# Residual base finished by VectorE in one operation in place of one of ScalarE and one of GpSimd, with all five queues of a two-layer graph network ordered anew

## The reference, cut to what matters

```python
h = jnp.maximum(_layernorm(x), 0.0)
x = x + L @ (h @ W + b)                    # layer 0; L is the normalised adjacency + I
h = jnp.maximum(_layernorm(x), 0.0)        # layer 1 starts
# hypergraph convolution: out = D^-1 H B^-1 H^T (h @ W^T) + bias, H = (adj != 0)
t = relu(hconv(h, adj, W1, b1))            # 512 -> 1024
t = layer_norm(t, gamma, beta)
x = x + (hconv(t, adj, W2, b2) + h)        # 1024 -> 512, plus the layer's own input
```

## Time and profile before

| | us |
|---|---|
| time, median of 3 runs | 1917.77 (1917.34 to 1918.89) |
| time of the profiled execution | 1915.19 |
| its span, first to last instruction | 1913.3 |
| TensorE busy | 1881.8 |
| VectorE busy | 1661.5 |
| ScalarE busy | 1450.5 |
| GpSimd busy | 1235.0 |
| mean granted TensorE clock | 0.998 |

### The profile page before, as it was taken

How to read it: one execution, slowest core, us unless ns; L and a number is a source line. 1 busy time by engine, 2 the same in 40 slices (tenths; PEclk the granted TensorE clock), 3 DMA queues, 4 the chain that set the end, 5 groups by cost and what they waited for, 6 DMA issues and landing times.

```text
span 1913.3 us, 37357 instructions
## 1 busy us (share of the span) xinstructions
PE 1881.8 (98%) x10104; PEld 911.1 (48%) x10104; DVE 1661.5 (87%) x3177; ACT 1450.5 (76%) x2726; POOL 1235.0 (65%) x1554
## 2 busy tenths in 40 slices
...
GB/s 231 58 105 96 108 115 90 106 116 84 108 112 90 108 115 90 108 113 91 108 112 91 107 112 91 108 111 90 111 103 98 111 103 99 111 95 99 83 66 78
DMA packets 518736, 197.65 MB, mean 103 GB/s; under 512 B 466816, under 2 KB 483328, under 8 KB 518528
## 3 DMA queue, kind: packets, MB, share of 16 engines
...
## 4 chain that ended last, share of the span: by engine, by line
PE 84%; issue 4%; DVE 4%; POOL 2%; DMA 1%; SPq 0%; ACT 0%; DVEq 0%; POOLq 0%
PE ps_u L405 31%; PE ps_e L405 15%; PE ps_x L416 15%; PE ps_z L416 7%; PE ps_y L416 4%; PE ps_y L456 1%; PE ps_y L458 1%; PE ps_y L457 1%; PE ps_t L393 1%; PE ps_t L394 1%; PE ps_t L395 1%; PE ps_e L456 1%; PE ps_e L458 1%; PE ps_e L457 1%; DMA raw_t<-bet_wide 1%
## 5 line engine op out<-in xcount | busy, mean ns | idle before, releaser
L405 PE MATMUL ps_u<-w2h,raw_t 128*128 128x512 f16 x2016 | 476.2, 379 | 0.0
L1506 POOL TENSOR_TENSOR base<-b_all,xh 128x512 f32<-128x512 f32 x128 | 210.9, 1647 | 353.7 <-DVE raw_w L1141 343.8
L405 PEld LDWEIGHTS ps_u<-w2h,raw_t 128*128 128x128 f16 x2016 | 194.6, 98 | 224.3 <-issue 0.8
L1083 DVE SCALAR_TENSOR_TENSOR raw_w<-ps_x,dn,b_all 128x512 f32<-128x512 f32 x192 | 141.9, 739 | 117.3 <-PE ps_x L416 116.9
L405 PE MATMUL ps_u<-w2l,raw_t 128*128 128x512 f16 x1008 | 238.1, 379 | 0.0
L788 ACT ACTIVATE bet_wide<-raw_w 128x1024 f16<-128x1024 f32 x128 | 134.2, 1048 | 78.8 <-DMA raw_t<-bet_wide 75.3
L1498 POOL TENSOR_TENSOR b_all<-x,b_all 128x512 f32<-128x512 f32 x128 | 167.0, 1305 | 16.7 <-DMA b_all<-in_b_dram 7.7
L1556 POOL TENSOR_SCALAR u<-ssq 128x2 f32<-128x2 f32 x64 | 34.1, 532 | 216.9 <-ACT raw_w L773 216.4
L1511 POOL TENSOR_TENSOR base<-base,raw_w 128x512 f32<-128x512 f32 x128 | 166.8, 1303 | 8.0
L779 ACT ACTIVATE raw_w<-raw_w,nm,sc 128x1024 f32<-128x1024 f32 x128 | 151.9, 1232 | 23.3 <-POOL nm L1582 23.3
L1127 DVE TENSOR_TENSOR bet_wide<-raw_w,bet_wide 128x1024 f16<-128x1024 f32 x128 | 158.7, 1240 | 7.2 <-ACT bet_wide L788 3.6
(11 more groups left out here) (178 smaller groups left out, 4901.3 us busy)
## 6 DMA issues: line engine op xcount, KB each, us to landing
x_t<-in_x_dram SPq DMA_DIRECT2D x128, 256.0 KB, 2.9
out_dram<-raw_w SPq DMA_DIRECT2D x128, 256.0 KB, 2.5
...
raw_t<-bet_wide SPq DMA_TRANSPOSE x256, 3.3
...
h0T_hi<-h_hi SPq DMA_TRANSPOSE x128, 2.5
h0T_lo<-h_lo SPq DMA_TRANSPOSE x128, 2.4
...
```

What stands on the lines that cost most here:

```text
L405: mm = pe.matmul(ps, t[:, j * 128:(j + 1) * 128], w[:, j, :], start=(n == 0 and j == 0), stop=(n == 2 and j == blocks - 1))
L1083: return dve.scalar_tensor_tensor(out=z, in0=bank[:, :], scalar=dn1[:, p % 2, j:j + 1], in1=z if row is None else row[:, cols], op0=ALU.mu ...
L1506: pool.tensor_tensor(base[:, g % 6, :], x1b[:, :], xh[:, g % 2, :], ALU.add).then_inc(s_scr2, 1)
```

## The change

The multiply by qdn and the add to base become one operation of VectorE. ScalarE's vq with its two buffers and its semaphore goes, GpSimd's base2 goes, and qdn waits for VectorE's base2 instead of vq.

```diff
-        vq = raw_w2[:, 4:6, :]
...
-            def do_vq(g):
-                p, j = g // 2, g % 2
-                act.wait_ge(s_qdn, p + 1)
...
-                done(act, s_base2, g - 1)
-                act.activation(vq[:, j, :], v_all[:, :], ACT.Copy, scale=qdn[:, p % 2, j:j + 1]).then_inc(s_vq, 1)
...
+            def do_base2(g):
+                p, j = g // 2, g % 2
+                dve.wait_ge(s_scr2, g + 1)
+                dve.wait_ge(s_qdn, p + 1)
+                if g == 0:
+                    dve.wait_ge(s_v, 1)
+                dve.scalar_tensor_tensor(out=base[:, g % 6, :], in0=v_all[:, :], scalar=qdn[:, p % 2, j:j + 1],
+                                         in1=base[:, g % 6, :], op0=ALU.mult, op1=ALU.add).then_inc(s_base2, 1)
...
-            def do_base2(g):
-                pool.wait_ge(s_vq, g + 1)
-                pool.wait_ge(s_scr2, g + 1)
-                pool.tensor_tensor(base[:, g % 6, :], base[:, g % 6, :], vq[:, g % 2, :], ALU.add).then_inc(s_base2, 1)
...
             def do_qdn(p):
...
-                done(pool, s_vq, 2 * p - 2)
+                done(pool, s_base2, 2 * p - 2)
```

All five queues are written anew. The loop starts at k = 12 in place of 4, and the pairs before are written out. In the start there are 208 `keep_busy` matmuls in place of 178, P(1), P(2) and the product beta_row stand earlier on TensorE, and VectorE scales and splits W1 before x1 of the first graphs. TensorE's start (all before M1 of pair 0) and its loop:

```diff
-            keep_busy(14, ps_u)
+            keep_busy(16, ps_u)
             gram_of_weight(0, raw_w0, range(0, 4))
-            keep_busy(18, ps_u)
+            keep_busy(32, ps_u)
             weight_sum(0, gram[:, 0, 0:N + 1])
-            keep_busy(60, ps_x)
+            keep_busy(38, ps_x)
             do_P(0)
+            keep_busy(37, ps_x)
+            do_P(1)
             gram_of_weight(1, raw_w1, range(0, 4))
-            do_Y0(0); do_Y0(1)
+            keep_busy(4, ps_x)
             weight_sum(1, gram[:, 1, 0:N])
-            keep_busy(10, ps_x)
-            do_Z0(0); do_P(1)
-            keep_busy(8, ps_x)
-            do_Z0(1); do_Y0(2)
+            keep_busy(4, ps_x)
+            beta_row(range(0, 2))
+            do_Y0(0); do_Y0(1); do_P(2)
+            beta_row(range(2, 4))
             weight_sum(2, wsq[:, 0:KH])
...
             for k in range(STEADY_FROM, STEADY_TO):
-                do_M1(k); do_Y0(2 * k + 5); do_U(2 * k - 3); do_M6(k); do_Y2(2 * k - 4); do_P(k+2); do_T1(2 * k + 2)
-                do_M7(k); do_Z0(2 * k + 5); do_M5(k); do_Y0(2 * k + 6); do_Y2(2 * k - 3); do_M3(k); do_M4(k)
-                do_M2(k); do_T1(2 * k + 3); do_U(2 * k - 2); do_Z0(2 * k + 6)
+                do_M1(k); do_Z0(2 * k + 6); do_P(k+2); do_U(2 * k - 3); do_Y0(2 * k + 7); do_M6(k); do_Y2(2 * k - 4)
+                do_T1(2 * k + 2); do_M7(k); do_M5(k); do_Y2(2 * k - 3); do_Z0(2 * k + 7); do_M3(k); do_M2(k)
+                do_Y0(2 * k + 8); do_M4(k); do_T1(2 * k + 3); do_U(2 * k - 2)
```

VectorE's loop:

```diff
             for k in range(STEADY_FROM, STEADY_TO):
-                do_x1(2 * k + 4); do_ul(2 * k - 4); do_st1(2 * k + 4); do_z1(k); do_ahat(k+7); do_aggr1(2 * k + 4)
-                do_bn0(2 * k + 8); do_yv(2 * k + 5); do_aggr0(2 * k + 8); do_tlS(k); do_yl(2 * k + 5)
-                do_h0_lo(2 * k + 6); do_h0_lo(2 * k + 7); do_z6(k); do_out(2 * k - 4); do_hn_lo(2 * k - 2)
-                do_ul(2 * k - 3); do_x1(2 * k + 5); do_st1(2 * k + 5); do_z5(k); do_aggr1(2 * k + 5); do_z7(k)
...
+                do_ul(2 * k - 4); do_z1(k); do_x1(2 * k + 6); do_w(k+4); do_cm(k+4); do_st1(2 * k + 6); do_inv(k+4)
+                do_aggr1(2 * k + 6); do_tlS(k); do_HB_hi(2 * k + 8); do_HB_hi(2 * k + 9); do_Hu(k+7)
+                do_h0_lo(2 * k + 8); do_HB_lo(2 * k + 8); do_bn0(2 * k + 10); do_HB_lo(2 * k + 9)
+                do_aggr0(2 * k + 10); do_h0_lo(2 * k + 9); do_A_lo(k+7); do_ul(2 * k - 3); do_ahat(k+8)
+                do_yv(2 * k + 7); do_z6(k); do_hn_lo(2 * k - 2); do_out(2 * k - 4); do_yl(2 * k + 7); do_z5(k)
+                do_out(2 * k - 3); do_z7(k); do_x1(2 * k + 7); do_dm(k+2); do_z3(k); do_st1(2 * k + 7); do_z2(k)
+                do_ri(k+2); do_hn_lo(2 * k - 1); do_P_lo(k+2); do_base2(2 * k + 2); do_base2(2 * k + 3)
+                do_yv(2 * k + 8); do_z4(k); do_bn0(2 * k + 11); do_yl(2 * k + 8); do_aggr0(2 * k + 11)
+                do_aggr1(2 * k + 7); do_dn(k+2); do_u0(k+5); do_xh_lo(k+2); do_tlA(k+1); do_nmu(k); do_dds(k+7)
```

GpSimd's loop:

```diff
             for k in range(STEADY_FROM, STEADY_TO):
...
-                do_nm2(k-1); do_scr2(2 * k + 2); do_x1b(2 * k + 3); do_base2(2 * k + 2); do_u1(k+2); do_sc1(k+2)
-                do_nm1(2 * k + 4); do_nm1(2 * k + 5); do_scr2(2 * k + 3); do_base2(2 * k + 3); do_x1b(2 * k + 4)
-                do_rd0(k+4); do_dn1(k+2); do_S3(k+1); do_qdn(k+2); do_cx(k+4); do_S1(k+1)
+                do_sc1(k+2); do_S2(k); do_nm1(2 * k + 4); do_S4(k); do_nm1(2 * k + 5); do_u2(k-1); do_dn2(k+1)
+                do_sc2(k-1); do_bias0(2 * k + 8); do_nm2(k-1); do_bias0(2 * k + 9); do_scr2(2 * k + 2)
+                do_x1b(2 * k + 3); do_scr2(2 * k + 3); do_x1b(2 * k + 4); do_S3(k+1); do_rd0(k+5); do_dn1(k+2)
+                do_qdn(k+2); do_cx(k+5); do_u1(k+3); do_S1(k+1)
```

More of the change, by code:

```diff
@@ new lines, in _ @@
+            beta_row(range(4, 6))
+            do_Y0(2); do_Z0(1)
+            beta_row(range(6, 8))
+            keep_busy(17, ps_x)
+            do_Z0(2)
+            keep_busy(6, ps_x)
+            do_Y0(3)
+            keep_busy(22, ps_x)
+            do_T1(0); do_Z0(3); do_T1(1)
+            keep_busy(32, ps_x)
+            do_Y0(4); do_M1(0); do_M2(0); do_M5(0); do_Z0(4); do_M6(0); do_P(3); do_Y0(5); do_M3(0); do_M7(0)
+            do_T1(2); do_M4(0); do_T1(3); do_Z0(5); do_Y0(6); do_M1(1); do_P(4); do_M2(1); do_M6(1); do_Z0(6)
@@ new lines, in _ @@
+            do_M3(NP - 11); do_M2(NP - 11); do_Y0(NG - 14); do_M4(NP - 11); do_T1(NG - 19); do_U(NG - 24)
+            do_M1(NP - 10); do_Z0(NG - 14); do_P(NP - 8); do_U(NG - 23); do_Y0(NG - 13); do_M6(NP - 10)
+            do_Y2(NG - 24); do_T1(NG - 18); do_M7(NP - 10); do_M5(NP - 10); do_Y2(NG - 23); do_Z0(NG - 13)
+            do_M3(NP - 10); do_M2(NP - 10); do_Y0(NG - 12); do_M4(NP - 10); do_T1(NG - 17); do_U(NG - 22)
+            do_M1(NP - 9); do_Z0(NG - 12); do_P(NP - 7); do_U(NG - 21); do_Y0(NG - 11); do_M6(NP - 9)
```

1048 lines of the change are left out of this document (570 added, 478 removed).

## The result

The changed kernel takes 1957.3 us, median of 4 runs (1955.05 to 1959.38), against 1917.55 us for the kernel before (4 runs, 1917.32 to 1918.89). The ratio is 1.0207, with a 95% interval of 1.0194 to 1.0219. It is slower by 40 us. The forecast was 1915.7 us, in a range of 1908 to 1929. The profiled execution took 1955.05 us with a span of 1953.2 us.

The account below looks back on a forecast made before the run. VectorE, with the loads before it, was taken to set the start and TensorE everything after. Start -3.6 and longer lead +1.5 made -2.1 us, taking the median from 1917.8 to 1915.7 us; range 1908 to 1929.

Parts of the forecast that it names:

- So it fits: Loop: VectorE's operations still meet TensorE's steps, so the period stays 28.77 us, with little room left.
- the 0.37 us counted: Loop: z6 ends 0.37 us before M7, and z5 0.37 us before M3.
- M1 of pairs 13 to 55 exactly 28.77 us apart (third rival if more): Loop test: M1 spacing of 28.77 us confirms the forecast; a longer spacing points to the third rival.
- The third rival: Loop: VectorE becomes the bound, late at z6 before M7; +15 us (1931) or, with locks, +28 (1944); chance 0.2.
- base2's cost: VectorE: each new base2 takes 0.65 us from start to start.
- VectorE's total: Whole kernel: VectorE's busy time goes to about 1745 us, 91%.
- The start: Up to U(3): VectorE sets it; U(3) starts at 152.5 us, with 3.6 us less loss than before.
- The count of VectorE's work: Start: VectorE has 143.5 us of work up to ul(2), which U(3) was said to wait for.
- The idle term: Start: VectorE idles 9 us up to ul(2), from a range of 7 to 15 us.
- TensorE's work ahead: Start: TensorE has 94.2 us of needed work ahead of U(3) in the new queue.
- The filling of the longer lead: Pairs between U(3) and the loop: 1.5 us added while VectorE's queue builds up its longer lead.
- The end: End of the kernel: order kept, so no change in time.

Follow-up runs that it names:

- runs 1: Changed kernel with eight buffers for the residual base in place of six: 2049.7 us.
- 12: Changed kernel with eight base buffers and both bias0 ahead of u2 on GpSimd in the loop: 1976.3 us.
- run 15: Against run 5, the start's base2(2) to (7) moved later on VectorE, behind ul(2), ul(3) and u0(7), with qdn(3) to (5) following on GpSimd: 1920.7 us.
- run 5: Changed kernel with both bias0 put ahead of u2 on GpSimd in 44 loop periods: 1921.6 us, 1.0016 to 1.0035 of the kernel before.

## Why the prediction was wrong

**The loop, the step that failed.** The prediction walked one period and concluded "So it fits". It compared z6 with M7, z5 with M3 and tlA with M1, that is, VectorE against TensorE, and took ScalarE and GpSimd as hidden, since their work per pair is below 28.77 us. Both halves fail. GpSimd's queue from rd0 to bias0 and ScalarE's from h0_hi to hn_hi are serial parts of a chain that runs through three engines and closes on itself, 29.57 us long. The slacks at M7 and M3 were there, though smaller than the 0.37 us counted (0.12 and 0.19 us in pair 22), and neither was the constraint. The sentence "M1 of pairs 13 to 55 exactly 28.77 us apart (third rival if more)" had the right test and the wrong reading: it was more, at neither M7 nor M3 first, but as a pause at U(2k-3). It also left ul before U out altogether, and had tlA end 0.8 us before M1, where it ended 0.09 before.

**The third rival** (chance 0.2) was the right side, but not the mechanism. It asked for 26.9 + 1.9 us of VectorE work or a wait for GpSimd ahead of z6. VectorE's work was 25.3 us. Its form of it, a collision with GpSimd ahead of z6, was met in runs 1 and 12 only.

**base2's cost** was 0.67 us from start to start (two from 737.70 to 739.03) against 0.65: right. What it took from ScalarE and GpSimd gained nothing, as forecast.

**VectorE's total** was forecast at 1745 us and came to 1664.1: wrong by the collisions that the new order avoids (yl, HB_lo and A_lo, 1.8 us per pair), which the sum carried on.

**The start, the second step that failed.** Forecast 3.6 us better, it came 2.8 us worse at U(3), which starts at 158.89 us: a loss of 64.7 against 61.9. The count of VectorE's work was right, 144.2 us measured at ul(2)'s end against 143.5. The idle term was mis-sized: 157.90 - 144.20 = 13.7 us in place of 9. TensorE's work ahead, 94.2 us, stands. So -3.6 became +2.8. But work and idle time do not give U(3), whatever their sizes: it starts 1.0 us after ul(2) ends, and it does not wait for it. The last matmuls of U(2), the first of Y0(11), the last of P(5) and the first of U(3), and then ul(2) on VectorE:

```profile
154.34 1.89 PE L418 MATMUL ps_u<-w2h,raw_t 128*128 128x512 f16 x8
156.07 1.03 PE L418 MATMUL ps_e<-w0h,h0T_hi 128*128 128x512 f16 x4
...
158.83 0.22 PE L482 MATMUL ps_p<-HB,A_HT 128*128 128x129 f16 x1
158.89 1.89 PE L418 MATMUL ps_u<-w2h,raw_t 128*128 128x512 f16 x8
...
157.26 0.68 DVE L1171 SCALAR_TENSOR_TENSOR raw_w<-ps_u,raw_w 128x512 f16<-128x512 f32 x1
```

TensorE goes from U(2) to U(3) without a pause. Its loss was 64.7 us already at M1(2), which starts at 122.36 us: the 36.5 us from there to U(3) are all needed work. So what VectorE did between 122 us and ul(2) did not set U(3). In the kernel before it is the same, with 61.8 us lost at M1(3), 150.81 us, and 61.9 at U(3); that ul(2) ended 0.2 us ahead of U(3) there was a coincidence, and the prediction built its sum on it. It also fits run 15: of the six base2 that were moved, (6) and (7) had stood at 128.9 and 148.7 us in run 5, behind TensorE's last wait, and taking the other four away left the loss at M1(2) as it was (64.2 against 63.9).

The 2.8 us come earlier. At M1(0) the new start is 4.7 us behind the old one (56.1 against 51.4), at M1(2) 3.6. TensorE's two longest waits before M1(0) are 2.83 us at T1(0), against 1.08 in the old start, and 2.54 us at Y0(4), for the DMA transpose of h0_hi(4), against 0.38. Which of its waits up to M1(2) decides was not tested, so what sets the new start stays open. The scatter is part of the difficulty: the kernels that have the new start unchanged had M1(0) at 71.7 to 77.7 us in their profiled executions.

**The filling of the longer lead**, +1.5 us for the pairs up to the loop, measured 2.4 from M1(5) to M1(12): a little more. **The end**, forecast 0, measured 1.8.
